# A gated attention and FFN block: the last score tile, the input statistics and the gate of the first pair are moved

## The reference

```python
xn = layernorm(x)
q, k, v = (gelu(xn @ W1) @ W2 for each of the three)
s = tril(q @ k.T / sqrt(256 * 512)) @ v
s = layernorm(s) * ln_w + ln_b
h = relu(xn @ sign-quantised W1 + b1)          # 1024 wide
g = silu(h @ sign-quantised W2 + b2)
out = x + s * g
```

## Time and profile before

| what | value |
|---|---|
| median of 3 runs | 309.47 us (308.98 to 310.45) |
| the profiled execution | 309.53 us |
| its span | 307.8 us |
| granted TensorE clock | 1.00 of full speed |
| TensorE busy | 98% of the span |
| VectorE, ScalarE, GpSimd busy | 81%, 72%, 44% |
| bytes moved | 19.06 MB, mean 62 GB/s |

### The profile page before, as it was taken

The page is one execution under the profiler, slowest core; times in us unless marked ns, Lnnn a source line. Parts: engine busy times, 40 slices in busy tenths (PEclk is TensorE's granted clock), DMA queues, the critical chain, the costliest instruction groups (busy, mean ns, idle before and its releaser), DMA issues.

```text
span 307.8 us, 5738 instructions
## 1 busy us (share of the span) xinstructions
PE 301.8 (98%) x1878; PEld 271.2 (88%) x1878; DVE 248.7 (81%) x545; ACT 221.1 (72%) x418; POOL 134.5 (44%) x104
## 2 busy tenths in 40 slices
PE   8999999999999999999999999999999999999993
PEld 8888899889988899888997889888998889988893
DVE  4999898957989588976989669895789858596686
ACT  3687948966785857949489576877579495795862
POOL 3852955067060942429151670609515291403100
PEclk9999999999999999999999999999999999999999
DMA  7960044310006000240004100060001500020001
GB/s 246 375 200 2 0 138 136 144 63 2 1 2 204 0 0 0 60 145 0 0 0 147 58 0 0 0 205 0 0 0 24 181 0 0 0 70 3 0 2 68
DMA packets 15228, 19.06 MB, mean 62 GB/s; under 512 B 1776, under 2 KB 12528, under 8 KB 15216
## 3 DMA queue, kind: packets, MB, share of 16 engines
q1 hardware_dynamic: 14656, 18.51, 18.5%
q10 hardware_dynamic: 560, 0.40, 0.4%
HBM read 14.69 MB, written 4.22 MB: 61 GB/s over the span
## 4 chain that ended last, share of the span: by engine, by line
PE 96%; DVE 2%; ACT 0%; issue 0%; POOL 0%
PE bank L803 93%; PE bank L794 2%; PE bank L787 1%; DVE gw L721 1%; DVE gw L612 0%; DVE x_all L614 0%; DVE gw L750 0%; DVE y L727 0%; ACT xT_hi L418 0%; POOL o_rstd L354 0%; ACT o_square L476 0%; ACT o_var L479 0%; DVE ones L507 0%
## 5 line engine op out<-in xcount | busy, mean ns | idle before, releaser
L702 DVE TENSOR_TENSOR r_lo<-bank,r_hi 128x512 fp32r<-128x512 f32 x64 | 43.9, 691 | 34.3 <-ACT bank L456 34.3
L455 ACT ACTIVATE r_hi<-bank,col 128x512 fp32r<-128x512 f32 x64 | 47.0, 735 | 23.4 <-PE bank L803 23.4
L354 POOL TENSOR_TENSOR o_rstd<-o_var,neg_half 128x2 f32<-128x2 f32 x16 | 11.2, 700 | 82.4 <-ACT o_var L479 82.4
L456 ACT ACTIVATE bank<-bank,col 128x512 f32<-128x512 f32 x64 | 45.5, 711 | 0.0
L315 POOL TENSOR_TENSOR y<-y,xn 128x512 f32<-128x512 f32 x12 | 20.4, 1704 | 55.6 <-DMA y<-in_x_t 55.6
L803 PE MATMUL bank<-xT_lo,w1q 128*128 128x512 f32 x128 | 39.9, 393 | 0.0
L803 PE MATMUL bank<-xT_hi,w1q 128*128 128x512 f32 x128 | 39.9, 393 | 0.0
L463 ACT CAST s_hi<-s 128x512 fp32r<-128x512 f32 (+3 forms) x32 | 14.7, 461 | 31.5 <-DVE s L690 28.7
L434 ACT ACTIVATE g_hi<-bank,col 128x512 fp32r<-128x512 f32 x48 | 33.9, 706 | 2.0 <-PE bank L803 1.5
L803 PE MATMUL bank<-w2q,r_lo 128*128 128x256 f32 x256 | 35.0, 279 | 0.0
L803 PE MATMUL bank<-w2q,r_hi 128*128 128x256 f32 x256 | 34.3, 276 | 0.0
(11 more groups left out here) (133 smaller groups left out, 704.8 us busy)
## 6 DMA issues: line engine op xcount, KB each, us to landing
out<-x_all SPq DMA_DIRECT2D x15, 256.0 KB, 3.2
x_all<-in_x SPq DMA_DIRECT2D x7, 512.0 KB, 3.6
xn<-x_norm_rows SPq DMA_DIRECT2D x6, 512.0 KB, 4.1
y<-in_x_t SPq DMA_DIRECT2D x6, 512.0 KB, 4.5
x_all<-in_w1t SPq DMA_DIRECT2D x2, 512.0 KB, 7.7
x_all<-in_w2t SPq DMA_DIRECT2D x1, 1024.0 KB, 10.5
row<-in_rows SPq DMA_DIRECT2D x1, 512.0 KB, 4.8
x_all<-in_x SPq DMA_DIRECT2D x1, 256.0 KB, 3.0
```

The lines of the kernel that those rows point to most:

```text
L354: nc.gpsimd.tensor_tensor(o_rstd[:, half], o_var[:, half], neg_half[:, half], ALU.pow).then_inc(o_rstd_made, 1)
L455: nc.scalar.activation(r["hi"][:, f], pre[:], ACT.Relu, bias=b1)
L456: nc.scalar.activation(pre[:], pre[:], ACT.Relu, bias=b1).then_inc(f1_whole, 1)
L702: nc.vector.tensor_tensor(r["lo"][:, f], bank[(AT_F1 + f) % BANKS][:], r["hi"][:, f].bitcast(FP32), ALU.subtract).then_inc(r_split, 1)
```

## The change

Four edits:

1. The last score tile (j = 3, 128 columns) is made by four products in place of six. The two parts of g become one buffer, so that z_hi meets g_hi and g_lo side by side in one product of 256 columns (two segments of 128) for each k; z_lo×g_hi stays at 128 columns. The bank then holds two partial sums. ScalarE copies the second (128 columns) to s32 after its last RELU, before its first `s_hi` cast; VectorE adds the first sum, d and the copy, and multiplies by the mask in a second instruction that waits for the first.
2. In batches 1 to 5 the four bn_stats for batch i + 2 stand between VectorE's `r_lo` 1 to 4; `x_statistics` keeps its waits and `aggregate`.
3. On VectorE, in all batches but the first and the last, the gate of the first pair stands ahead of `y_bias` of Y2 and `o_scale(1)`; its addition stays behind them.
4. On GpSimd, in the same batches, `offset(0)` stands ahead of `o_rstd_of(1)`.

The new semaphores `s_part_copied` and `s_part_made` are declared besides.

```diff
         x_mean_all, x_rstd_all = (x_norm_all.rearrange("q (p n t) -> q n t p", n=2, t=TT)[:, n] for n in range(2))
         xT = {"hi": sb("xT_hi", [P, CK, T], FP32R), "lo": sb("xT_lo", [P, CK, T], FP32R)}
         raw_qkv = sb("raw_qkv", [P, 6, CK, C])
-        g = {"hi": sb("g_hi", [P, 6, T], FP32R), "lo": sb("g_lo", [P, 6, T], FP32R)}
+        g_both = sb("g", [P, 2, 6, T], FP32R)
+        g = {"hi": g_both[:, 0], "lo": g_both[:, 1]}
         r = {"hi": sb("r_hi", [P, FT, T], FP32R), "lo": sb("r_lo", [P, FT, T], FP32R)}
         z = {"hi": sb("z_hi", [P, CK, T], FP32R), "lo": sb("z_lo", [P, CK, T], FP32R)}
 
...
                                             ALU.add).then_inc(s_made, 1)
 
                 o_rstd_of(0)
+                if not (first or last):
+                    offset(0)
                 o_rstd_of(1)
+                if first:
+                    offset(0)
                 if not last:
-                    offset(0)
                     offset(1)
                     if not second_last:
                         x_rstd_of(i + 2)
...
                 if first:
                     act.wait_ge(v_read, 2)
                     nc.scalar.copy(v["hi"][:], v32[:]).then_inc(v_hi_made, 1)
+                act.wait_ge(s_summed, 4 * i + 4)
+                if first:
+                    act.wait_ge(w2_quantized, 1)
+                else:
+                    act.wait_ge(s_split, 4 * i)
+                nc.scalar.copy(s32[:, S_AT[TT - 1]:S_AT[TT - 1] + P],
+                               bank[(AT_S + TT - 1) % BANKS][:, P:2 * P]).then_inc(s_part_copied, 1)
                 for j in range(TT):
                     act.wait_ge(s_read, 4 * i + j + 1)
                     at = slice(S_AT[j], S_AT[j] + S_COLS[j])
...
                 dve.wait_ge(steps, ready + 5)
                 nc.vector.scalar_tensor_tensor(var, part[:, 2], 1.0 / C, part[:, 3], ALU.mult, ALU.add).then_inc(made, 1)
 
-            def x_statistics(b, second=False):
+            def x_tile_stats(b, t):
+
+                nc.vector.bn_stats(x_stats[:, t], x_all[:, b, t]).then_inc(x_stats_made, 1)
+
+            def x_statistics(b, second=False, made=False):
 
                 dve.wait_ge(x_loaded, 16 * b)
                 if not second:
                     dve.wait_ge(xn1_made, TT)
                     dve.wait_ge(x_norm_stored, 16 * b - 32)
-                for t in range(TT):
-                    nc.vector.bn_stats(x_stats[:, t], x_all[:, b, t]).then_inc(x_stats_made, 1)
+                if not made:
+                    for t in range(TT):
+                        x_tile_stats(b, t)
                 aggregate(x_stats, x_part, x_mean, x_var, x_stats_made, STEPS * (b - 1) + TT, x_var_made)
 
             def x_statistics0():
...
                                     apply_absolute_value=True).then_inc(abs1_summed[0], 1)
 
             def batch(i, first=False, second_last=False, last=False):
-                def finish(b, t, tiles, n):
+                def gate(b, t, tiles, n):
                     part = slice(t, t + tiles)
                     dve.wait_ge(s_made, 2 * b + (1 if t == 0 else 2))
                     dve.wait_ge(silu_made, 2 * b + n)
                     nc.vector.tensor_tensor(gw[:, part], gw[:, part], y[:, part], ALU.mult).then_inc(s_gated, 1)
+
+                def add_x(b, t, tiles, n):
+                    part = slice(t, t + tiles)
                     dve.wait_ge(s_gated, 2 * b + n)
                     nc.vector.tensor_tensor(x_all[:, b, part], x_all[:, b, part], gw[:, part],
                                             ALU.add).then_inc(out_made, 1)
+
+                def finish(b, t, tiles, n):
+                    gate(b, t, tiles, n)
+                    add_x(b, t, tiles, n)
 
                 def g_lo(p):
                     m = ORDER[p]
...
 
                     dve.wait_ge(s_summed, 4 * i + j + 1)
                     src = bank[(AT_S + j) % BANKS]
+                    if j == TT - 1:
+                        at = slice(S_AT[j], S_AT[j] + P)
+                        dve.wait_ge(s_part_copied, i + 1)
+                        nc.vector.scalar_tensor_tensor(s32[:, at], src[:, 0:P], d[:, j:j + 1], s32[:, at],
+                                                       ALU.add, ALU.add).then_inc(s_part_made, 1)
+                        dve.wait_ge(s_part_made, i + 1)
+                        nc.vector.tensor_tensor(s32[:, at], s32[:, at], causal[:], ALU.mult).then_inc(s_read, 1)
+                        return
                     last_op = nc.vector.scalar_tensor_tensor(s32[:, S_AT[j]:S_AT[j] + P], src[:, 0:P], d[:, j:j + 1],
                                                              causal[:], ALU.add, ALU.mult)
                     if S_COLS[j] > P:
...
 
                 for f in range(FT):
                     r_lo(f)
+                    if not (first or second_last or last) and 1 <= f <= TT:
+                        if f == 1:
+                            dve.wait_ge(x_loaded, 16 * i + 32)
+                        x_tile_stats(i + 2, f - 1)
                 dve.wait_ge(d_summed, i + 1)
                 for t in range(TT):
                     at = slice(t * P, (t + 1) * P)
...
                     y_bias(AT_Y0, 0, 2, 3 * i + 1)
                     y_bias(AT_Y1, 2, 1, 3 * i + 2)
                     if not second_last:
-                        x_statistics(i + 2)
+                        x_statistics(i + 2, made=not first)
                     o_scale(0)
                     if first:
                         xT_lo(1, [bank[(AT_X1 + k) % BANKS][:] for k in range(CK)])
+                    if not first:
+                        gate(i, 0, 2, 1)
                     y_bias(AT_Y2, 3, 1, 3 * i + 3)
                     o_scale(1)
-                    finish(i, 0, 2, 1)
+                    if first:
+                        gate(i, 0, 2, 1)
+                    add_x(i, 0, 2, 1)
                 else:
                     def offset(h):
                         half = slice(2 * h, 2 * h + 2)
...
                 split_product(claim(i, AT_D)[:], [(ones_r[:], e[part][:]) for part in ("lo", "hi")]).then_inc(d_summed, 1)
 
                 pe.wait_ge(z_split, 2 * i + 2)
-                for j in range(TT):
+                for j in range(TT - 1):
                     dst = claim(i, AT_S + j)
                     split_product(dst[:, 0:S_COLS[j]], [(z[a][:, k, j * P:(j + 1) * P], g[b][:, k, j * P:T])
                                                         for a, b in FULL for k in range(CK)]).then_inc(s_summed, 1)
+                dst = claim(i, AT_S + TT - 1)
+                tail = slice(T - P, T)
+                both = [g_both[:, :, k, tail] for k in range(CK)]
+                sums = dst[:, 0:2 * P].rearrange("p (a t) -> p a t", a=2)
+                nc.tensor.matmul(sums, z["hi"][:, 0, tail], both[0], start=True, stop=False)
+                for k in range(CK):
+                    nc.tensor.matmul(dst[:, 0:P], z["lo"][:, k, tail], g["hi"][:, k, tail], start=False, stop=False)
+                nc.tensor.matmul(sums, z["hi"][:, 1, tail], both[1], start=False, stop=True).then_inc(s_summed, 1)
 
                 def weighted_sums():
 
```

More of the change, by code:

```diff
@@ L165, in gated_block @@
         v_hi_made, v_split = sem("v_hi_made"), sem("v_split")
-        s_hi_made, s_split = sem("s_hi_made"), sem("s_split")
+        s_hi_made, s_split, s_part_copied, s_part_made = (
+            sem("s_hi_made"), sem("s_split"), sem("s_part_copied"), sem("s_part_made"))
         silu_made, s_made, s_gated = sem("silu_made"), sem("s_made"), sem("s_gated")
```

## The result

The changed kernel takes 311.45 us (median of 8 runs, 310.42 to 311.97) against 309.63 for the kernel before beside it: a ratio of 1.0048, 95% interval 1.0033 to 1.0063, so 1.0 to 2.0 us slower, 1.5 in the middle. Forecast: 310.4 us, 0.3% slower. The profiled execution took 311.26.

A forecast was written before the change was run, and what follows sets the result against it. TensorE, 98% busy, bounds the kernel now; after the change a loop without its throughput does. Batches 1 to 5 +0.8, batch 0 0, batch 6 -0.1, last batch +0.15: +0.85, so 310.4 us, range 308.6 to 311.8.

The forecast's parts named there:

- the loop without TensorE: Chain from stage V through RELU, scores, y_bias, gate, GELU to g_lo 5 and V: 0.16 us longer than a batch takes now.
- Six products to four: Last score tile on TensorE: two weight loads fewer, 0.115 us each, save 0.23 us per batch, bounds 0 and 0.35.
- ScalarE's copy, 0, and the dependent step, +0.33: Tile 3's score: the copy costs nothing; VectorE's second instruction takes 0.29 plus 0.04 wait, making s_read(3) 0.33 us later.
- Y_bias of Y2 0.67 late: VectorE, batch 1: behind the gate, which waits for offset(0), y_bias of Y2 starts at 86.73 instead of 86.06 us.
- G_lo 5, +0.16: VectorE's sixth g_lo, awaited by stage V's opening weight load, ends at 96.85 instead of 96.69 us, 0.16 later.
- TensorE waits some 0.4 us at V: Stage V's opening weight load waits about 0.4 or 0.5 us for g_lo; batches take 36.3 to 36.4.
- Batch 6, -0.1: Without x statistics its o_scale(0) follows TensorE's sums, so it keeps perhaps half of the 0.23 us saving: -0.1.
- Batches 1 to 5, +0.8: Each of the five batches gets 0.16 us longer: 5 x 0.16 = +0.8 us.
- A: Rival: TensorE's gain comes through if the gate delays y_bias of Y2 by at most about 0.3; 308.1 us, chance 0.13.
- B: Rival: the effects cancel, the loop past TensorE being as long as now; 309.5 us, chance 0.2.
- C: Rival: clearly slower, waits at tile 3 and gate 0.13 instead of 0.04; 0.39 per batch, 311.5 us, chance 0.22.
- D: Rival: the four products save nothing, only columns count; changes nothing in the forecast, no case or chance of its own.

The follow-up runs named there:

- e5: Kernel before with only the four products, ScalarE's copy and VectorE's two steps for tile 3; statistics, gate and offset(0) in their old places: 308.72 us, 0.9971.
- e6: Kernel before with only the four bn_stats moved between the low halves of RELU: 309.95 us, 1.0005.
- e10: Changed kernel with a third dependent 128x128 VectorE step in tile 3's score, which changes no number: 312.24 us, 1.0076.
- e9: e8 with tile 3 of the last batch as in the kernel before (six products, no copy, one VectorE step): 308.23 us, 0.9947.
- e2: Changed kernel with the first pair's gate moved behind y_bias of Y2, still ahead of o_scale(1); GpSimd's order as in the change: 308.94 us, 0.9972.
- e8: e2 with TensorE's wait at Y0 split: Y0 starts with r_lo 6, r_lo 7 is awaited only at the product reading it: 307.83 us, 0.9935.
- e4: Changed kernel without the four products: six products in one sum, no ScalarE copy, one VectorE step for tile 3: 309.49 us, 0.9993.
- e3: Changed kernel with six products in the last score tile again, still in two sums, copy and two VectorE steps kept: 310.87 us, 1.0041.
- e1: Changed kernel with the first pair's gate and GpSimd's offset(0) back in their old places: 309.11 us, 0.9977.
- e11: e8 with one more dependent VectorE step of the same size in tile 3's score: 308.83 us, 0.9966.

## Why the prediction was right, step by step

The forecast's mechanism and place were right: the loop without TensorE became the bound, by way of the gate's wait for offset(0). Measured 0.48% slower for 0.27% forecast (from the median of 309.47 the sum of +0.85 gives 310.3, not 310.4). Step by step:

- **Six products to four, -0.23 per batch.** Right: the tile takes 0.46. A 128-column product costs its weight load, 0.11 us, not its columns. The Trainium skill's "TensorE: Matmul & The Clock Gate" gives 107 ns for 128 columns in its section "LDWEIGHTS", and the 0.11 between loads agrees. By the isolated gap of its section "Back-to-back issue gap" nothing would have been saved, and the trace decides against that here. The forecast left out that the same section says that in a stream of load and product pairs both set the distance, some 81 ns at 128 columns; the first half fits the trace, the figure does not (0.115 us). Alone the edit is worth 0.9 us (`e5`).
- **The bn_stats, 0.** Right (`e6`: 1.0005): one of 0.42 in each slot of 0.47, r_lo 7 on time.
- **ScalarE's copy, 0, and the dependent step, +0.33.** `e10`'s third step, of the same shape, puts 0.33 between starts (81.03 - 80.70), and o_scale(0) of `e5` is 0.33 late.
- **Y_bias of Y2 0.67 late.** Measured 11.98 - 11.33 = 0.65. Two errors in it cancel: s_scale(0) starts 0.12 later than I had it (open, see the end), and from the first y_bias to o_scale(0) it takes 1.63 where I summed 1.75. The idle time ahead of the gate was forecast as 1.4 (1.40), the gate as 0.7 (0.69).
- **G_lo 5, +0.16.** Measured 22.12 - 21.96 = 0.16 in batches 2 to 5, 0.39 in batch 1 (22.36), whose s_scale(0) is 0.36 late.
- **"TensorE waits some 0.4 us at V", and with it a batch of 36.3 to 36.4.** Size of the batch right (36.25 to 36.37; 36.60 in batch 1), but I had taken TensorE's products as unchanged behind the wait. V's first product comes only 0.2 to 0.4 late (0.6 in batch 2), and V and F1 are longer by 0.32 in three of five batches and by 0.10 in two. This hid in the sum because in the kernel before V already followed a wait of 0.24 (V took 2.81 to 2.90 there, F1 up to 7.47): the widening was mostly in the 36.20 already.
- **Batch 6, -0.1.** Measured 35.80 instead of 36.16, -0.36: it doesn't wait at all, so it gets the whole undisturbed length. Mis-sized by 0.26, to the good side.
- **Batches 1 to 5, +0.8.** +0.61 over batches 1 to 6, less batch 6's -0.36, is +0.97, of which batch 1 has 0.38 (36.60 - 36.22). Forecast 0.2 too low, by batch 1.
- **The last batch, +0.15.** 0.12 in the profile, 0.13 by `e9`.
- **Batch 0, 0.** -0.11 from R to R, inside its bounds; the 1.12 in front of the first R go with the clock's rise.

By the traces the change is +0.62 (-0.11 + 0.97 - 0.36 + 0.12) against a forecast of +0.85; the runs say +1.5, 1.0 at the least. That the sum of the traces comes within 0.2 is in part luck, since batch 1 errs one way and batches 6 and 0 the other. Most of the 1.0 us between the forecast's 310.4 and the measured 311.45 is not in the traces.

**The rivals.** A (the gain comes through, 308.1 us) is what happens once y_bias of Y2 is freed from the gate: `e2` 308.94 and `e8` 307.83. Its condition, the gate no more than 0.3 in y_bias's way, was the right one. B (309.5) has the time of `e4` (309.49): without tile 3's second step the loop without TensorE is even shorter than before (g_lo 5 at 21.79 for 21.96), and TensorE sets the 36.01. C needed waits of 0.13 where I had 0.04: the trace shows 0.04 (80.45 + 0.34 = 80.79 to 80.83; 86.02 + 1.29 = 87.31 to the gate's 87.34), so it falls, though its 311.5 lies as near to the measured 311.45 as a time can. D holds in `e3` as stated: in the forecast's regime products don't count. As a claim about TensorE it falls by `e5`, and by the 36.01 of `e4` against the 35.80 of `e8`.

The best version is `e8`: four products, bn_stats between the low halves, offset(0) first on GpSimd, the gate behind y_bias of Y2, and Y0's wait for r_lo 7 placed at its reader. It is 0.65% below the kernel before (0.4 to 0.9).

## What to carry to other kernels

With TensorE 98% busy, a saving on it counts only as long as no loop that runs past it becomes the longer one: write each such loop out, and look which instruction in it a moved wait now stands ahead of. Here one wait ahead of a 0.42 us bias cost 2.4 us, and the same wait one instruction later nothing. Put a wait on the instruction that reads the data, not on its stage's first one, and test edits together and apart: the parts here measured -0.9, +0.2 and +5.2 us alone, +1.5 together.

## What the runs showed of the hardware that was not expected

- **A late weight load can cost more than its wait.** Behind some of them products are spaced 0.118 instead of 0.113 us (256 columns) and 0.233 instead of 0.229 (512), for two to five stages on: 0.42 us behind the load at Y0 in `e2`'s batches 2 and 4, 0.32 behind the one at V in three of five batches of the changed kernel. The granted clock is 1.00 throughout and TensorE counts as busy. Not every late load does it: in five batches of `e5` the load at Y0 starts 0.12 after r_lo 7, as in those of `e2`, and Y0 and Y1 take 5.47, not 5.67; `e3` waits 0.4 to 0.6 at V and its F1 takes 7.33 in every batch. What decides, and why the distance stays wide, is open; with the wait moved to the reader (`e8`) it did not occur.
- **Full clock comes between 4.1 and 7.3 us** after the span's start, whatever the kernel, with TensorE doing the same 44 products: 1.1 us of difference between the two profiles that is nobody's edit.
- **A gap of 0.12 us (0.36 in batch 1) ahead of s_scale(0)** on VectorE is there in all versions with edits 1 and 2 together (the changed kernel, `e1`, `e2`, `e3`, `e8`, `e9`), not with either alone, and gone with one instruction more in the batch (`e10`, `e11`). What it comes from is open; no run tests it by itself.
